# The last column block's second product in five rounds of 8 row tiles, with the closing of each group between rounds

## The chip, the cores and the metric

The kernel runs on one core of one Trainium2 chip. The metric is device time in microseconds (us) of one execution. Engines by their names in the profile: PE (TensorE, matrix product), PEld (its weight loads), DVE (VectorE), ACT (ScalarE), POOL (GpSimd), SP (SyncE, which issues most transfers here). SBUF is the on-chip memory, PSUM the accumulators that PE writes (8 banks of 512 f32 columns per partition, taken here as 4 pairs).

## The reference

`x` is 5120x64, `adj` a sparse 5120x5120 f32 matrix. What matters here, cut down:

```python
e = concat([par_u0*par_u1*(diag_u*x_u @ W_u) + x_u, par_i0*par_i1*(diag_i*x_i @ W_i) + x_i])
h = adj @ (adj.T @ e)
out = layernorm(h) * gamma + beta + x
x1 = layernorm(x + out)
result = layernorm(x1 + graph_layers(x1, adj))
```

`graph_layers` keeps edges and nodes by thresholds. A largest row-wise sum of squares of `adj` under a bound proves that nothing survives them; then the second part adds zero, and the last line is a layer norm of a layer norm. The kernel computes that maximum, stores the short answer, and branches on the flag at its very end; with these inputs the branch is not taken.

## The kernel before, in words

**Tiling.** The 5120 rows are 40 row tiles of 128. The columns of `adj` come in 11 blocks (`NB`), two of 256 columns and nine of 512. A block arrives in units of 1024 elements per partition (two row tiles of a 512-column block). For each block PE first multiplies all its tiles against `e` (`multiply_unit`, L1303, the product `adj.T @ e`). ACT sums the squares of each unit, and DVE transposes each unit in 32x32 squares (`turn_unit`, L1159). The product's two halves are transposed (`turn_half`), spread over the partitions by PE (`spread_block`, L1318) and copied to SBUF by ACT (`keep_cols`, L1069).

**Second product and rounds.** `multiply_round` (L1333) then multiplies the transposed tiles by the block's 64 columns of `adj.T @ e`. One round takes some of the row tiles: 16, 16 and 8 (`ROUND_TILES`). A round writes four PSUM banks, one for each quarter of the partitions, 32 output columns for each row tile; all 16 column groups of the block accumulate there. `add_round` (L1180) on DVE adds the four banks into `h_sum` in SBUF. So `h_sum` is complete for a row tile once the last block's round with that tile has been added. In the blocks before the last, PE alternates a round of block c with units of block c+1, so that all waits on adds lie behind other products.

**Banks.** Rounds write banks 0 to 3, the last two rounds of the program banks 4 to 7 (`round_banks`). A round waits until the round before it has been added (`round_added`); the second round of the last block waits only for one older, since it takes the other four banks.

**Closing.** The 40 tiles are closed in five groups of 8 (`GT`, `LGROUPS`). `close_tiles(k)` (L1346) multiplies 8 tiles of `h_sum` by a fixed centering matrix into a PSUM pair (`nat_of`: pairs 0, 1, 0, 1, 2). Then for each group k, with the name and line of each step:

- ACT squares the centered values: `square_c` (L1091)
- DVE sums and scales them: `sum_c` (L1209, L1211)
- POOL takes the power -0.5: `root_c` (L1022)
- DVE multiplies and adds the prepared `x`: `make_y` (L1217, L1221); the first of the two frees the PSUM pair (`t_made`)
- ACT squares again: `square_y` (L1096)
- DVE sums: `sum_y` (L1227, L1230)
- POOL takes the power: `root_y` (L1027)
- DVE scales: `make_out` (L1238)
- SP stores 256 KB (L967)

Each engine works its own list in the order that the code has; an instruction whose semaphore is late holds everything behind it on that engine. The order in which the steps of the five groups follow each other on DVE, ACT and POOL is written out by hand.

Of the kernel before, what the change touches and what calls it, by code (L numbers as in the profile page):

```python
# [7 lines left out]
def adjacency_layers_kernel(nc, x, adj, w_ui, diag, par, gamma, beta,  # L8
# [38 lines left out]
    ROUND_TILES = (16, 16, 8)  # L47
    ROUND_FIRST = (0, 16, 32)
    RPB = len(ROUND_TILES)
    NR = NB * RPB  # L50

# [28 lines left out]
    with ctx:  # L80
# [42 lines left out]
        assert ln_at + 8 * GT * D <= x_at + SLOT * ROUND_TILES[0] * CH // SLOT  # L123
# [194 lines left out]
        def units_of_round(g):  # L318

            c, j = g // RPB, g % RPB  # L320
            first, last = ROUND_FIRST[j], ROUND_FIRST[j] + ROUND_TILES[j]
            return range(UNIT_FIRST[c] + first // UNIT_TILES[c], UNIT_FIRST[c] + last // UNIT_TILES[c])
# [10 lines left out]
        def round_of_tile(t):  # L333
            return 0 if t < 16 else 1 if t < 32 else 2

        def round_of_unit(v):
            c, i = place_of_unit(v)
            return RPB * c + round_of_tile(UNIT_TILES[c] * i)

# [11 lines left out]
        def round_banks(g):  # L351

            return bank[4:8] if g >= NR - 2 else bank[0:4]

# [4 lines left out]
        def turned_of(g):  # L359

            c, j = g // RPB, g % RPB
            at, w, nt = SLOT * SLOT_FIRST[c] + WIDTHS[c] * ROUND_FIRST[j], WIDTHS[c], ROUND_TILES[j]
            return pooled[:, at:at + w * nt].rearrange("p (t b r) -> p t b r", b=w // 32, t=nt)

        def h_of(j):


            at, nt = ROUND_FIRST[j] * P, ROUND_TILES[j]
            return h_sum[:, at:at + nt * P].rearrange("p (t a r) -> p a t r", a=QUADS, t=nt)
# [571 lines left out]
        def _(sp):  # L941
            for k in range(LGROUPS):
                sp.dma_start(x_first[:, group_tiles(k), :], tile_rows(x, GT * k, GT)).then_inc(x_loaded[k], 16)
            for v in range(UNITS):
# [9 lines left out]
                if before:  # L954
                    sp.wait_ge(round_done, round_of_unit(before[-1]) + 1)
# [5 lines left out]
            sp.wait_ge(round_done, RPB * (NB - 2) + 1)  # L961
# [12 lines left out]
        def _(pool):  # L974
# [69 lines left out]
        def _(act):  # L1044
# [17 lines left out]
            def keep_cols(c):  # L1062
                act.wait_ge(cols_spread, c + 1)
                if c >= 2:
                    act.wait_ge(round_done, RPB * (c - 1))
# [53 lines left out]
        def _(dve):  # L1119
# [49 lines left out]
            def add_round(g):  # L1169
                j, w = g % RPB, 32 * ROUND_TILES[g % RPB]  # L1170
                dve.wait_ge(round_done, g + 1)
                if g >= RPB:
                    dve.wait_ge(round_added, g - RPB + 1)
                for a in range(QUADS):
                    to = h_of(j)[:, a, :, :]
                    share = round_banks(g)[a][:, 0:w].rearrange("p (t r) -> p t r", r=32)
                    if g < RPB:
# [14 lines left out]
            for g in range(NR - RPB):  # L1192
                for i, v in enumerate(units_of_round(g + RPB)):
                    if i == 1 and g % RPB == RPB - 1:
                        turn_half(g // RPB + 1)
                    turn_unit(v)
                if g == NR - RPB - 2:
# [5 lines left out]
            add_round(NR - 3)  # L1203
            add_round(NR - 2)

# [64 lines left out]
        def _(pe):  # L1270
# [51 lines left out]
            def multiply_round(g):  # L1322
                w, to, kb = 32 * ROUND_TILES[g % RPB], turned_of(g), WIDTHS[g // RPB] // 32
                pe.wait_ge(unit_turned, units_of_round(g).stop)
                if g % RPB == 0:
                    pe.wait_ge(cols_kept, g // RPB + 1)
# [102 lines left out]
```

## Time and profile before

| | us |
|---|---|
| median of 3 runs (lowest, highest) | 430.44 (429.62, 434.01) |
| the profiled execution | 430.32 |
| its span, first to last instruction | 428.5 |
| PE busy | 393.6 |
| DVE busy | 329.3 |
| ACT busy | 229.3 |
| POOL busy | 39.4 |

Starts are counted from the first instruction of the span. An engine's busy time is a sum over its instructions, not a claim that it sets the time; the chain of waits is the view that follows, from the last instruction back, what each step was released by. One f32 matmul of the program shows as two matmuls and two weight loads in the trace, so a round of 64 matmuls is x128 there.

### The profile page before, as it was taken

The page shows a single profiled execution, that of the slowest core. Times are in us where ns is not written, and L with a number is a line of the kernel's source. Part 1 is how long each engine was busy: PE and PEld are TensorE (multiplying, and loading weights), DVE is VectorE, ACT ScalarE, POOL GpSimd, SP SyncE. Part 2 cuts the span into 40 slices and gives each one's busy share as a digit, 9 for nine tenths or more (in the row PEclk, how much of TensorE's full clock was granted, in tenths as well). Part 3 has the DMA queues.
Part 4 walks back from the last instruction along what each step waited for, and adds up shares of the span by engine and source line. Part 5 has one row for each costly group of instructions (what it writes and reads, how often), then busy time and mean ns, then how long its engine had stood idle before and what let it go on. Part 6 is the DMA issues. An engine that isn't in the chain of part 4 may idle for free.

```text
span 428.5 us, 13460 instructions
## 1 busy us (share of the span) xinstructions
PE 393.6 (92%) x5872; PEld 233.0 (54%) x5872; DVE 329.3 (77%) x404; ACT 229.3 (54%) x439; POOL 39.4 (9%) x56
## 2 busy tenths in 40 slices
PE   4997999999999999999999999999899999989910
PEld 3884665555565464555546456554545655455900
DVE  1588999998796796978679697967769796953864
ACT  2368579398079239607923960990396098010310
POOL 5000000000000000000000000000000000294473
PEclk9998999999999999999999999999999999999975
DMA  7999999967795795979379597957939793000012
GB/s 232 349 349 366 386 386 386 387 244 280 271 386 170 281 377 208 351 267 363 119 284 376 212 348 268 364 193 264 392 142 342 276 365 128 2 4 2 3 49 79
DMA packets 61984, 109.84 MB, mean 256 GB/s; under 512 B 3936, under 2 KB 14304, under 8 KB 61920
## 3 DMA queue, kind: packets, MB, share of 16 engines
q1 hardware_dynamic: 61248, 108.80, 71.3%
q8 instruction: 48, 0.79, 0.8%
q10 hardware_dynamic: 672, 0.12, 0.1%
q14 instruction: 16, 0.13, 0.1%
HBM read 107.60 MB, written 1.31 MB: 254 GB/s over the span
## 4 chain that ended last, share of the span: by engine, by line
PE 89%; DVE 3%; POOL 3%; issue 2%; DMA 1%; ACT 1%; DVEq 0%
PE pair L1303 42%; PE pair L1333 41%; PE pair L1318 3%; PE pair L1288 2%; POOL pooled L1027 2%; POOL pooled L1022 2%; PE pair L1278 1%; DMA pooled<-in_x 1%; PE pair L1346 1%; DVE pooled L1217 0%; DVE pooled L1159 0%; DVE pooled L1238 0%; DVE pooled L1227 0%; DVE pooled L1178 0%; DVE pooled L1180 0%
## 5 line engine op out<-in xcount | busy, mean ns | idle before, releaser
L1159 DVE STREAM_TRANSPOSE pooled<-pooled 128x1024 f32<-128x1024 f32 x200 | 229.9, 1207 | 7.7 <-PE pair L1303 4.7
L1059 ACT ACTIVATE scratch<-pooled 128x1024 bf16<-128x1024 f32 x200 | 208.2, 1050 | 0.0
L1333 PE MATMUL pair<-pooled,col_sum 32*64 32x512 f32 (+1 forms) x3840 | 181.0, 520 | 5.3 <-issue 3.2
L1303 PE MATMUL pair<-pooled,rows_in 128*64 128x256 f32 (+1 forms) x1760 | 183.6, 367 | 0.0
L1303 PEld LDWEIGHTS pair<-pooled,rows_in 128*64 128x64 f32 x1760 | 121.3, 140 | 67.4 <-issue 18.9
L1333 PEld LDWEIGHTS pair<-pooled,col_sum 32*64 32x64 f32 x3840 | 84.3, 132 | 88.2 <-issue 81.0
L1180 DVE TENSOR_TENSOR pooled<-pooled,pair 128x512 f32<-128x512 f32 (+1 forms) x120 | 63.4, 588 | 64.9 <-PE pair L1333 64.9
L1069 ACT COPY col_sum<-pair 128x512 f32<-128x512 f32 (+1 forms) x22 | 11.0, 550 | 138.2 <-PE pair L1318 138.2
L1059 ACT ACTIVATION_READ_ACCUMULATOR scratch<-pooled 128x1 f32 x200 | 38.9, 195 | 0.0
L1008 POOL TENSOR_SCALAR pooled<-pooled 128x40 f32<-128x40 f32 x1 | 0.3, 316 | 363.3 <-DVE pooled L1199 363.3
L1318 PE MATMUL pair<-col_half,spread_cols 64*128 64x256 f32 (+1 forms) x88 | 11.6, 383 | 3.8 <-DVE col_half L1167 3.8
L1091 ACT ACTIVATE pooled<-pair 128x512 f32<-128x512 f32 x5 | 3.0, 593 | 18.8 <-PE pair L1346 18.8
L1318 PEld LDWEIGHTS pair<-col_half,spread_cols 64*128 64x128 f32 x88 | 7.2, 186 | 10.0 <-issue 5.7
L1096 ACT ACTIVATE pooled<-pooled 128x512 f32<-128x512 f32 x5 | 3.1, 630 | 14.9 <-DVE pooled L1221 14.9
L1346 PEld LDWEIGHTS pair<-center,pooled 128*128 128x128 f32 x80 | 9.1, 192 | 1.2 <-issue 1.2
L1278 PE MATMUL pair<-ident,pooled 128*128 128x128 f32 x20 | 5.0, 403 | 5.1 <-DMA pooled<-in_x 5.1
L1133 DVE TENSOR_TENSOR rows_in<-pair,pooled 128x256 f32<-128x256 f32 x10 | 3.8, 419 | 7.7 <-PE pair L1288 7.7
L1346 PE MATMUL pair<-center,pooled 128*128 128x128 f32 x80 | 9.5, 278 | 0.0
L1022 POOL TENSOR_TENSOR pooled<-pooled,minus_half 128x8 f32<-128x8 f32 x5 | 8.2, 1644 | 8.6 <-DVE pooled L1211 8.5
L1027 POOL TENSOR_TENSOR pooled<-pooled,minus_half 128x8 f32<-128x8 f32 x5 | 8.1, 1636 | 8.7 <-DVE pooled L1230 8.7
L1053 ACT COPY pooled<-pair 128x512 f32<-128x512 f32 x5 | 2.9, 585 | 11.0 <-PE pair L1278 11.0
L1288 PE MATMUL pair<-pooled 64*128 64x64 f32 x80 | 8.1, 366 | 0.6 <-ACT pooled L1053 0.6
(49 smaller groups left out, 74.8 us busy)
## 6 DMA issues: line engine op xcount, KB each, us to landing
pooled<-in_adj SPq DMA_DIRECT2D x200, 512.0 KB, 8.9
pooled<-in_x SPq DMA_DIRECT2D x5, 256.0 KB, 5.2
out<-pooled SPq DMA_DIRECT2D x5, 256.0 KB, 2.0
pooled<-in_x SPq DMA_DIRECT2D x1, 768.0 KB, 6.8
pooled<-in_x SPq DMA_DIRECT2D x1, 512.0 KB, 4.2
pooled<-in_w_ui ACTq DMA_DIRECT2D x2, 32.0 KB, 5.5
beta_sb<-in_beta ACTq DMA_DIRECT2D x1, 32.0 KB, 6.3
pooled<-in_diag ACTq DMA_DIRECT2D x1, 20.0 KB, 5.1
```

Source lines behind the costliest of these rows:

```text
L1022: nc.gpsimd.tensor_tensor(rstd[:, group_tiles(k)], var[:, group_tiles(k)], minus_half[:, :], ALU.pow).then_inc(rstd_made, 1)
L1027: nc.gpsimd.tensor_tensor(scale[:, group_tiles(k)], y_var[:, group_tiles(k)], minus_half[:, :], ALU.pow).then_inc(scale_made, 1)
L1059: nc.scalar.activation(scratch[v % 2][:, :], slots[slot_of(v)], ACT.Square, accum_out=square_sum[:, v:v + 1]).then_inc(unit_scanned, 1)
L1069: kept = act.copy(to.rearrange("p b (f i) -> p f b i", f=2), spread_bank[h][:, 0:w].rearrange("p (f b i) -> p f b i", f=2, i=32))
L1159: nc.vector.transpose(tiles, tiles).then_inc(unit_turned, 1)
L1180: added = nc.vector.tensor_tensor(to, to, share, ALU.add)
L1278: mm = pe.transpose(pair_bank(k)[:, P * j:P * j + P], x_first[:, t:t + 2, :].rearrange("p t d -> p (t d)"), ident[:, :])
L1288: mm = pe.matmul(xw_bank(k, odd)[:, t % GT // 2, :], xt_pairs[half(odd), P * (t // 2):P * (t // 2) + P], w_ui_sb[half(odd), D * w:D * w + ...
L1303: mm = pe.matmul(block_bank[c % 2][half(h), 0:w // 2], rows_in[:, t, :], slots[slot_of(v)][:, at:at + w // 2], start=(t == 0), stop=(t == ...
L1318: mm = pe.matmul(spread_bank[h][:, w * f:w * (f + 1)], spread_cols[f][half(h), :], col_half[half(h), 0:w], start=True, stop=True)
L1333: mm = pe.matmul(round_banks(g)[a][half(b % 2), 0:w].rearrange("p (t r) -> p t r", r=32), col_sum[g // RPB % 2][quadrant(a), b, :], to[qua ...
L1346: mm = pe.matmul(nat_of(k)[:, i, :], h_sum[:, P * t:P * t + P], center[:, :], start=True, stop=True)
```

## The change

The last block's rounds are five of 8 row tiles; the other ten blocks keep 16, 16 and 8. Round and group sizes in the last block are now equal: group k closes the tiles of its round k. On PE, `close_tiles(0)` stands behind round 1, `close_tiles(1)` behind round 2, `close_tiles(2)` behind round 3, and 3 and 4 behind round 4. The last block's rounds 1 to 4 all write banks 4 to 7, round 0 banks 0 to 3. The order of the closing steps on DVE, ACT and POOL is rewritten to match. The rest of the diff replaces arithmetic on round numbers by tables and changes no instruction.

```diff
-    ROUND_TILES = (16, 16, 8)
-    ROUND_FIRST = (0, 16, 32)
-    RPB = len(ROUND_TILES)
-    NR = NB * RPB
+    PARTS = ((0, 16), (16, 16), (32, 8))
+    LAST_PARTS = tuple((t, 8) for t in range(0, T, 8))
+    RPB = len(PARTS)
+    ROUNDS_AT = [RPB * c for c in range(NB)]
+    LAST = ROUNDS_AT[NB - 1]
+    NR = LAST + len(LAST_PARTS)
...
+        def place_of_round(g):
+
+            c = min(g // RPB, NB - 1)
+            return (c,) + (LAST_PARTS if c == NB - 1 else PARTS)[g - ROUNDS_AT[c]]
...
+        def rounds_through(c, t):
+
+            return next(g + 1 for g in range(NR) if place_of_round(g)[0] == c and t < sum(place_of_round(g)[1:]))
...
-            return bank[4:8] if g >= NR - 2 else bank[0:4]
+            return bank[4:8] if g > LAST else bank[0:4]
...
             root_c(0)
             root_c(1)
             root_y(0)
+            root_c(2)
             root_y(1)
-            root_c(2)
             root_c(3)
+            root_c(4)
             root_y(2)
-            root_c(4)
             root_y(3)
             root_y(4)
...
             square_y(0)
-            square_y(1)
             act.wait_ge(c_summed, 1)
             square_c(2)
+            square_y(1)
             act.wait_ge(c_summed, 2)
...
-            add_round(NR - 3)
-            add_round(NR - 2)
+            add_round(LAST)
+            add_round(LAST + 1)
...
             sum_c(0)
+            add_round(LAST + 2)
+            make_y(0)
             sum_c(1)
-            make_y(0)
+            sum_y(0)
+            add_round(LAST + 3)
             make_y(1)
-            add_round(NR - 1)
-            sum_y(0)
+            make_out(0)
+            sum_c(2)
             sum_y(1)
-            sum_c(2)
+            add_round(LAST + 4)
+            make_y(2)
+            make_out(1)
             sum_c(3)
-            make_out(0)
-            make_out(1)
-            make_y(2)
+            sum_y(2)
+            sum_c(4)
             make_y(3)
-            sum_c(4)
-            sum_y(2)
+            make_y(4)
             sum_y(3)
-            make_y(4)
             make_out(2)
+            sum_y(4)
             make_out(3)
-            sum_y(4)
...
-                if g == NR - 2:
+                if g == LAST + 1:
                     pe.wait_ge(round_added, g - 1)
                 elif g:
                     pe.wait_ge(round_added, g)
...
-                pe.wait_ge(round_added, NR - RPB + round_of_tile(GT * k) + 1)
+                pe.wait_ge(round_added, rounds_through(NB - 1, GT * (k + 1) - 1))
...
-            multiply_round(NR - 3)
-            multiply_round(NR - 2)
+            multiply_round(LAST)
+            multiply_round(LAST + 1)
             close_tiles(0)
+            multiply_round(LAST + 2)
             close_tiles(1)
-            multiply_round(NR - 1)
+            multiply_round(LAST + 3)
             close_tiles(2)
+            multiply_round(LAST + 4)
             close_tiles(3)
             close_tiles(4)
```

PE's list from the last `spread_block` on, before (L1318 spreads, L1333 is the second product, L1346 closes, L1390 is the matmul for the maximum):

```order
L1318 MATMUL pair<-col_half,spread_cols 128x256 x4
L1333 MATMUL pair<-pooled,col_sum 64x512 x128
L1346 MATMUL pair<-center,pooled 128x128 x16
L1333 MATMUL pair<-pooled,col_sum 64x256 x64
L1346 MATMUL pair<-center,pooled 128x128 x24
L1390 MATMUL pair<-ident,part_max 1x128
```

The same place in the changed kernel, whose lines are L1324, L1340, L1353 and L1399:

```order
L1324 MATMUL pair<-col_half,spread_cols 128x256 x4
L1340 MATMUL pair<-pooled,col_sum 64x256 x128
L1353 MATMUL pair<-center,pooled 128x128 x8
L1340 MATMUL pair<-pooled,col_sum 64x256 x64
L1353 MATMUL pair<-center,pooled 128x128 x8
L1340 MATMUL pair<-pooled,col_sum 64x256 x64
L1353 MATMUL pair<-center,pooled 128x128 x8
L1340 MATMUL pair<-pooled,col_sum 64x256 x64
L1353 MATMUL pair<-center,pooled 128x128 x16
L1399 MATMUL pair<-ident,part_max 1x128
```

The first two closings moved ahead of rounds, one round later each, and only two closings are left behind the last round, where there were three.

DVE's list from the add of the last round on, before:

```order
L1180 TENSOR_TENSOR pooled<-pooled,pair 128x8x32 x4
L1227 TENSOR_REDUCE pooled<-pooled 128x8
L1230 TENSOR_SCALAR pooled<-pooled 128x8
...
L1209 TENSOR_REDUCE pooled<-pooled 128x8
L1211 TENSOR_SCALAR pooled<-pooled 128x8
...
L1238 TENSOR_TENSOR pooled<-pooled 128x512 x2
L1217 TENSOR_TENSOR pooled<-pair,pooled 128x512
L1221 TENSOR_TENSOR pooled<-pooled 128x512
```

And in the changed kernel (the add is L1183, `make_y` L1221 and L1225, `make_out` L1242, `sum_c` L1213 and L1215):

```order
L1183 TENSOR_TENSOR pooled<-pooled,pair 128x8x32 x4
L1221 TENSOR_TENSOR pooled<-pair,pooled 128x512
L1225 TENSOR_TENSOR pooled<-pooled 128x512
L1242 TENSOR_TENSOR pooled<-pooled 128x512
L1213 TENSOR_REDUCE pooled<-pooled 128x8
L1215 TENSOR_SCALAR pooled<-pooled 128x8
```

Behind the last add stood two `sum_y`, two `sum_c`, two `make_out` and only then the third group's `make_y`; now that `make_y` follows the add at once.

## Rows read from the trace of the kernel before

**Rows 1.** The page: the span, an instruction queue, and the chain's shares by engine

```profile
span 428.5 us, 13460 instructions
...
q8 instruction: 48, 0.79, 0.8%
...
PE 89%; DVE 3%; POOL 3%; issue 2%; DMA 1%; ACT 1%; DVEq 0%
```

**Rows 2.** The chain of waits, 372 us to the end: start, us, what

```profile
375.16 3.64 PE pair L1333 x128
...
381.09 13.99 PE pair L1333 x256
395.08 3.78 PE pair L1346 x32
...
398.88 0.61 ACT pooled L1091
...
405.78 3.23 POOL pooled L1027 x2
409.01 3.21 POOL pooled L1022 x2
```

**Rows 3.** Busy time by stretch: PE, PEld, DVE, ACT, POOL, granted clock, DMA share, GB/s

```profile
381.00:408.10 27.10, 27.01 (x466) 18.64 (x466) 13.83 (x29) 3.65 (x6) 14.29 (x12) 1.00 0.01 2
408.10:428.50 20.40, 0.25 (x2) 0.00 (x0) 10.66 (x21) 2.37 (x4) 10.58 (x7) 0.59 0.18 67
```

**Rows 4.** DVE's timeline: start, us, instruction, idle time before it and its releaser

```profile
395.17 2.48 DVE L1180 TENSOR_TENSOR pooled<-pooled,pair 128x512 f32<-128x512 f32 x4 [4.39 <-PE pair L1333]
397.73 0.69 DVE L1209 TENSOR_REDUCE pooled<-pooled 128x8 f32<-128x512 f32 x1
398.45 0.17 DVE L1211 TENSOR_SCALAR pooled<-pooled 128x8 f32<-128x8 f32 x1
...
401.13 0.69 DVE L1221 TENSOR_TENSOR pooled<-pooled 128x512 f32<-128x512 f32 x1
...
403.49 1.40 DVE L1180 TENSOR_TENSOR pooled<-pooled,pair 128x256 f32<-128x256 f32 x4
...
423.77 0.69 DVE L1238 TENSOR_TENSOR pooled<-pooled 128x512 f32<-128x512 f32 x1 [1.39 <-POOL pooled L1027]
```

**Rows 5.** POOL's and ACT's timeline in the closing stage

```profile
398.70 3.43 POOL L1022 TENSOR_TENSOR pooled<-pooled,minus_half 128x8 f32<-128x8 f32 x2 [8.50 <-DVE pooled L1211]
418.53 1.64 POOL L1027 TENSOR_TENSOR pooled<-pooled,minus_half 128x8 f32<-128x8 f32 x1
401.86 0.63 ACT L1096 ACTIVATE pooled<-pooled 128x512 f32<-128x512 f32 x1 [2.38 <-DVE pooled L1221]
```

**Rows 6.** PE's timeline around its waits, with one add of DVE

```profile
35.88 3.47 PE L1303 MATMUL pair<-pooled,rows_in 128*64 128x128 f32 x32
50.26 1.97 PE L1303 MATMUL pair<-pooled,rows_in 128*64 128x128 f32 x32
50.44 2.48 DVE L1178 COPY pooled<-pair 128x512 f32<-128x512 f32 x4 [0.23 <-PE pair L1333]
53.07 1.99 PE L1333 MATMUL pair<-pooled,col_sum 32*64 32x256 f32 x64 [0.84 <-DVE pooled L1178]
188.44 3.70 PE L1333 MATMUL pair<-pooled,col_sum 32*64 32x256 f32 x127
193.78 0.43 PE L1333 MATMUL pair<-pooled,col_sum 32*64 32x256 f32 x1 [1.63 <-issue]
305.38 0.37 PE L1333 MATMUL pair<-pooled,col_sum 32*64 32x256 f32 x1 [1.60 <-issue]
```

**Rows 7.** Busy time by stretch, as in Rows 3, for the clock behind two idle times

```profile
31.00:35.20 4.20, 0.48 (x10) 0.24 (x6) 4.20 (x6) 3.33 (x8) 0.00 (x0) 1.00 1.10 348
35.24:39.20 3.96, 3.96 (x40) 3.59 (x40) 2.48 (x3) 3.20 (x7) 0.00 (x0) 0.62 1.09 360
...
53.07:57.00 3.93, 3.93 (x86) 2.98 (x88) 3.87 (x8) 1.25 (x3) 0.00 (x0) 1.00 1.05 386
```

More of the change, by code:

```diff
@@ L316, in place_of_unit, with units_of @@
             return c, v - UNIT_FIRST[c]
[L318 to L322, printed above, removed]
+        def place_of_round(g):
+            c = min(g // RPB, NB - 1)
+            return (c,) + (LAST_PARTS if c == NB - 1 else PARTS)[g - ROUNDS_AT[c]]
+        def units_of(c, first, nt):
+            return range(UNIT_FIRST[c] + first // UNIT_TILES[c], UNIT_FIRST[c] + (first + nt) // UNIT_TILES[c])
         def tile_rows(ap, t0, nt):
@@ L954, in _ @@
                 if before:
-                    sp.wait_ge(round_done, round_of_unit(before[-1]) + 1)
+                    b, ib = place_of_unit(before[-1])
+                    sp.wait_ge(round_done, rounds_through(b, UNIT_TILES[b] * ib))
                 sp.dma_start(slots[slot_of(v)].rearrange("p (t k) -> p t k", t=ut),
@@ L1064, in keep_cols @@
                 if c >= 2:
-                    act.wait_ge(round_done, RPB * (c - 1))
+                    act.wait_ge(round_done, ROUNDS_AT[c - 1])
                 w, kb = WIDTHS[c], WIDTHS[c] // 64
@@ L1169, in add_round @@
             def add_round(g):
-                j, w = g % RPB, 32 * ROUND_TILES[g % RPB]
+                c, first, nt = place_of_round(g)
                 dve.wait_ge(round_done, g + 1)
-                if g >= RPB:
-                    dve.wait_ge(round_added, g - RPB + 1)
+                if c:
+                    dve.wait_ge(round_added, rounds_through(c - 1, first + nt - 1))
                 for a in range(QUADS):
-                    to = h_of(j)[:, a, :, :]
-                    share = round_banks(g)[a][:, 0:w].rearrange("p (t r) -> p t r", r=32)
-                    if g < RPB:
+                    to = h_of(first, nt)[:, a, :, :]
+                    share = round_banks(g)[a][:, 0:32 * nt].rearrange("p (t r) -> p t r", r=32)
+                    if c == 0:
                         added = nc.vector.tensor_copy(to, share)
@@ L1191, in _ @@
             turn_unit(UPB[0] - 1)
[L1192 to L1195, printed above, removed]
+            for g in range(LAST):
+                c, first, nt = place_of_round(g)
+                for i, v in enumerate(units_of(c + 1, first, nt)):
+                    if i == 1 and first + nt == T:
+                        turn_half(c + 1)
                     turn_unit(v)
-                if g == NR - RPB - 2:
+                if g == LAST - 2:
                     dve.wait_ge(x_again, 16 * 2)
@@ L1322, in multiply_round @@
             def multiply_round(g):
[L1323 to L1326, printed above, removed]
-                if g == NR - 2:
+                c, first, nt = place_of_round(g)
+                w, to, kb = 32 * nt, turned_of(g), WIDTHS[c] // 32
+                pe.wait_ge(unit_turned, units_of(c, first, nt).stop)
+                if first == 0:
+                    pe.wait_ge(cols_kept, c + 1)
+                if g == LAST + 1:
                     pe.wait_ge(round_added, g - 1)
@@ L1367, in _ @@
                     pe.matmul(bank[6][:, 0:D], center_t, center_g, start=True, stop=True).then_inc(gamma_turned, 1)
-            for g in range(NR - RPB):
-                c, j = g // RPB, g % RPB
-                ahead = units_of_round(g + RPB)
-                first = 2 if c == 0 else 0
-                if j == 0:
-                    for v in ahead[:first]:
-                        multiply_unit(v)
+            for g in range(LAST):
+                c, first, nt = place_of_round(g)
+                ahead = units_of(c + 1, first, nt)
+                early = 2 if g == 0 else 0
+                for v in ahead[:early]:
+                    multiply_unit(v)
+                if first == 0:
                     spread_block(c)
-                for v in ahead[first if j == 0 else 0:]:
+                for v in ahead[early:]:
                     multiply_unit(v)
```

21 lines of the change are left out of this document (8 added, 13 removed).

## The prediction

> **What bounds the kernel now.** I read the page first. The span is 428.5 us and PE holds 89% of the chain that ended last [rows 1], so up to the last block only PE's time matters. The chain of waits, read in order of time, shows where that ends [rows 2]. The last block's first two rounds run from 381.09 us for 13.99 us, two closings follow for 3.78 us, and from 398.88 us on PE is hardly in it: the chain goes through ACT, POOL (two pairs of powers, 3.23 and 3.21 us) and DVE. The busy times by stretch say the same [rows 3]: PE is busy 27.01 of 27.10 us up to 408.10 us and 0.25 us of the 20.40 us behind. In those 20.40 us, POOL is busy 10.58 us and DVE 10.66 us, so neither is full, but they hand work to each other. The last instruction starts at 423.77 us and takes 0.69 us [rows 4]: it ends at 424.46 us, 16.4 us behind PE's last closing.
>
> The question is therefore how soon the closing chains begin, and how many stand behind PE's end. POOL's first power starts at 398.70 us, after 8.50 us of waiting [rows 5]. There are ten powers at 1.6 us each, 16 us of POOL's time, of which two were done before PE's last closings began.
>
> **The change part by part.**
>
> *The rounds.* A 512-column round is 13.99/2 = 7.00 us, an 8-tile round 3.64 us [rows 2]. The old three make 7.00 + 7.00 + 3.64 = 17.64 us, the new five 5 x 3.64 = 18.20 us: **0.6 us more** on PE. Halving the long one would give 3.50 us, the lower bound; the row of the same shape is nearer, so I take 3.64.
>
> *The adds.* An add of 16 tiles is 2.48 us, one of 8 tiles 1.40 us [rows 4]. Five are 7.0 us against 2 x 2.48 + 1.40 = 6.4 us, 0.6 us more on DVE. It waits in this stretch (4.39 us in front of one add [rows 4]), so this costs nothing by itself. Without that cover it would cost 0.6 us.
>
> *The new waits.* Rounds 2, 3 and 4 take the banks that the round before them has just left, so each waits for an add that begins only when that round ends. The wait was behind two closings, now it is behind one. A closing is 3.78/2 = 1.89 us [rows 2]. An add starts 0.1 us after its round (395.08 to 395.17 us [rows 2, 4]), takes 1.40 us, and PE resumes 0.15 us after it (50.44 + 2.48 = 52.92, then 53.07 us [rows 6]): 1.65 us. It fits under 1.89 us with **0.24 us to spare**, if DVE is free when the round ends. Queued behind the waiting round is everything on PE; queued behind a waiting add on DVE are `make_y` and `sum_c` of the group before.
>
> *The walk.* I lay out every instruction of the closing stage in its engine's written order, at its row's duration. An 8-tile `sum` gives its result after 0.88 us and holds DVE for 0.8 us (397.73 to 398.45, plus 0.17), POOL starts 0.1 us later (398.70), a power is 1.64 us and holds POOL for 1.60 us, `make_y` is 1.41 us, ACT's squares 0.61 and 0.63 us, `make_out` 0.69 us [rows 2, 4, 5]. Done for the old order, this walk ends at 424.56 us; the trace has 424.46 us. That is my reason to trust it to some tenths. For the new order:
>
> - PE: rounds end at 384.7, 388.4, 393.9, 399.4 and 405.0 us, with closings between. The last closing ends at 408.7 us (408.2 in the same walk of the old order), without a wait.
> - DVE's adds start at 384.8, 388.5, 394.0, 399.5 and 405.1 us, each as its round ends. DVE is free for each; the narrowest is the last, free 0.7 us before.
> - POOL: the powers of group 0 start at 392.0 us, not at 398.7. Those of `root_c` 1, `root_y` 0, `root_c` 2 and `root_y` 1 start at 397.6, 399.2, 403.8 and 405.4 us, so **five of ten** have begun before PE is done.
> - After PE: closing 3 ends at 406.85, its square at 407.6, its sum starts at 408.3 (behind `make_y` and `make_out`), and `root_c` 3 starts at 409.3. From 410.9 us `root_c` 4 and `root_y` 2 to 4 run nearly back to back, to 418.1 us. The last `make_out` runs from 418.13 to 418.82 us.
>
> The end of DVE's work moves from 424.56 to 418.82 us, **5.7 us earlier**. What follows it (the store, the flag, the branch) has no changed instruction and moves as a whole. So the profiled execution of 430.32 us becomes 430.32 - 5.7 = **424.6 us**. It stands 0.12 us below the median of 430.44 us, so the same number holds for a median.
>
> *What is late next.* Behind 408.7 us, one group alone needs two squares, two sums, two powers, `make_y` and `make_out`: about 8.8 us with the handovers. The walk has 10.1 us there. The other 1.3 us is POOL's queue of groups 2 and 3 ahead of group 4.
>
> *Bounds.* With 3.50 us a round, the end comes 0.7 us earlier: 423.9 us. Each delay of a round moves the end by as much, since in the walk PE is always the engine that the adds wait for. An add that starts or hands over 1 us later costs 0.76 us at each of three rounds, plus the last: 3.3 us in the walk, 427.9 us.
>
> **One rule against the change.** Two instructions of mine on DVE read two SBUF operands, the second half of `make_y` (L1221) and `make_out` (L1238), and in the new order more of them run beside a POOL power. The row of L1221 at 401.13 us ran while POOL was in its pair of powers from 398.70 us for 3.43 us, and took 0.69 us [rows 4, 5], the same as the last L1238, which ran alone. So I charge nothing. The Trainium skill, page "SBUF — State Buffer", section "SBUF: two separate sides", says that such a DVE operation and a GpSimd one share a port pair under an exclusive lock, and that the one that comes second "fully blocks". By that rule this row would have been longer or later; the trace does not agree. It is a rival below.
>
> **The rivals**
>
> - **Late adds (0.10).** DVE is strictly in order and now has sums and multiplies ahead of the adds of rounds 2 to 4; if they are late, PE waits three times. For: only 0.24 us of slack at each. Against: in the walk DVE is free 0.7 to 2.2 us before each add. With 0.5 to 1 us at each, the walk gives 426.0 to 427.9 us.
> - **A hole in PE's instruction supply (0.13).** Twice PE stood for 1.63 and 1.60 us for no reason that the trace shows, both times before the last matmul of an 8-tile round, x127 and then x1 [rows 6]. An 8-tile round uses as many instructions as a 16-tile one in half the time, and the page has a queue that brings instructions [rows 1]. Five such rounds now stand close together. For: 2 of the 9 8-tile rounds of 512-column blocks had it. Against: both fell in stretches with heavy transfers, and the last 8-tile round, with next to none (2 GB/s [rows 3]), had none. One hole costs 1.6 us: 426.2 us.
> - **The tail keeps its length (0.06).** If what bounds the end were POOL's and DVE's hand-to-hand work as such, and not its start, the 16.4 us behind PE would stay, and the time would be 430.32 + 0.6 = 430.9 us. For: POOL and DVE are each half idle there. Against: eight powers stood behind 405 us before, five stand behind 409 us now.
> - **The port lock (0.03).** Four of the DVE operations with two SBUF operands (`make_y` 3 and 4, `make_out` 2 and 3) would each wait for the rest of a power, at most 1.64 us: 424.6 + 6.6 = 431.2 us at most.
> - **The clock falls: slower (0.03).** PE now changes between rounds and closings seven times in place of three. If it idled enough between them, its clock would fall from 2.4 to 1.2 GHz. What the rows show of that: after 3.75 us of waiting before 35.24 us the granted clock of the next stretch was 0.62, and 32 matmuls took 3.47 us that took 1.97 us later, 1.76 times [rows 6, 7]; after 0.84 us of waiting it stayed 1.00 [rows 6, 7]. In the walk PE does not wait at all, and the old stretch, which changes groups too, ran at 1.00 [rows 3]. Each microsecond of PE's work at the low level costs 0.76 us, so it decides from 5.7/0.76 = 7.5 us on. With all 20.4 us behind 388.4 us at that level: 424.6 + 15.5 = 440.1 us. The Trainium skill, page "TensorE: Matmul & The Clock Gate", section "A second HAM failure mode: psum-queue depth-cycling", tells of a kernel that cycles through PSUM banks whose clock swings for such small idle times; no run here shows it.
> - **Better than the walk (0.05).** Shorter rounds, or handovers under 0.1 us: 423.6 us.
>
> **How the numbers follow.** The forecast has 0.60 and spans 423.9 to 425.7 us by the bounds above. The low end of the range is 423.6, the high end 427.2 us: it takes in the hole and most of the late adds, and leaves out about 0.15. One per cent, about what a measurement of this kernel can tell, is 426.1 us for faster and 434.7 us for slower. Faster: 0.60 + 0.05, half of the hole and a quarter of the late adds, 0.74. Slower: the clock and a little for what I have not thought of, 0.04. The same: 0.22.
>
> **What would show it.** Five rounds of about 3.64 us each, with PE's last closing near 408.7 us, confirm the first step; waits of rounds 2 to 4 on L1183 refute the 0.24 us. POOL's first power near 392.0 us and its last from 416.5 us confirm the walk. DVE's last instruction near 418.1 us confirms the sum. A closing chain that follows PE's end by over 12 us, a wait named "issue" of over 1 us inside a round, or a granted clock below 1.00 before 408 us would each make the prediction wrong.

## The result

The changed kernel takes 426.46 us (median of 20 runs, 423.8 to 432.06) against 430.28 us (median of 20 runs of the kernel before). The ratio is **0.9913, 95% interval 0.9888 to 0.9937**: 3.7 us less, between 2.7 and 4.8. The ratio leaves out three executions of the changed kernel that were more than 1.5% above its fastest. The forecast was 424.6 us in a range of 423.6 to 427.2 us, 5.7 us less. The direction and the range held; the size was half as large again as it should have been, and lies outside the interval. The prediction had also drawn a line at one per cent, and gave 0.74 to a gain beyond it and 0.22 to none that large: measured, the gain is 0.87%, between 0.6% and 1.1%, so the smaller of these chances came out. The profiled execution took 426.81 us.

Three rows of the page of the changed kernel, the answer to [rows 1]:

```profile
span 425.0 us, 13984 instructions
...
q8 instruction: 50, 0.82, 0.8%
...
PE 91%; DVE 3%; issue 2%; POOL 2%; DMA 1%; ACTq 0%; ACT 0%
```

The span fell from 428.5 to 425.0 us, 3.5 us. The chain of waits of the changed kernel, the answer to [rows 2] (L1340 is the second product, L1353 closes, L1183 adds, L1025 and L1030 are the powers, L1242 is `make_out`):

```profile
381.04 7.17 PE pair L1340 x256
388.20 1.98 PE pair L1353 x16
390.19 3.64 PE pair L1340 x128
...
401.76 3.72 PE pair L1340 x128
...
405.55 0.29 issue
405.85 1.08 DVE pooled L1183 x3
...
409.73 3.25 POOL pooled L1025 x2
...
415.30 3.62 POOL pooled L1030 x2
418.92 0.02 issue
418.95 0.69 DVE pooled L1242
```

The last block starts at 381.04 us where it started at 381.09. A short round is 3.64 us, as in the forecast. A closing is 1.98 us, not 1.89. The last operation of DVE starts at 418.95 us, not at 418.13. After it there are 425.0 - 419.64 = 5.4 us to the end of the span; before the change these were 428.5 - 424.46 = 4.0 us.

The busy times by stretch, the answer to [rows 3] (PE, PEld, DVE, ACT, POOL, granted clock, DMA share, GB/s):

```profile
388.00:409.50 21.50, 21.19 (x474) 17.93 (x466) 15.26 (x36) 4.40 (x8) 10.24 (x7) 1.00 0.04 15
409.50:425.00 15.50, 0.00 (x0) 0.00 (x0) 8.28 (x18) 1.62 (x3) 8.45 (x5) 0.65 0.19 72
```

PE is as full as before while it alternates between rounds and closings, at a granted clock of 1.00, which is 2.4 GHz. The stretch with next to nothing on PE is 15.5 us, from 20.4.

**A measure for the experiments.** The first product of the last block starts anywhere from 378.9 to 383.8 us in the profiles shown here, for reasons that lie before anything that was changed. So each profile is measured below from that start, and of each run the ratio to the kernel before, timed beside it, is given. "Slower" means that the 95% interval of that ratio lies above 1; all ratios here lie within 2% of 1.

| kernel | start of last block | to the start of DVE's last operation | to the end of the span | SyncE's waits for the last stores |
|---|---|---|---|---|
| before | 381.09 | 42.68 | 47.41 | 2.0 |
| changed | 381.04 | 37.91 | 43.96 | 3.3 |
| e1 rounds alone | 381.16 | 46.62 | 51.64 | 2.3 |
| e2 order alone | 380.96 | 38.29 | 43.04 | 1.4 + 0.7 |
| e3 flag early | 378.89 | 39.19 | 43.91 | 2.1 |
| e4 sum first | 383.54 | 37.88 | 43.86 | 3.3 |
| e5 before, flag later | 381.56 | 42.72 | 49.04 | 3.6 |
| e6 adds delayed | 383.84 | 38.19 | 43.96 | 3.1 |
| e7 best, five rounds | 380.26 | 37.41 | 42.84 | 0.6 + 1.9 |
| e8 best, old rounds | 383.09 | 38.76 | 43.61 | 2.1 |
| e9 flag and buffers | 381.27 | 38.04 | 42.83 | 2.0 |
| e10 changed, again | 383.15 | 37.77 | 43.95 | 3.5 |
| e11 order alone, again | 380.93 | 38.29 | 43.07 | 1.1 + 1.0 |
| e12 best, again | 383.13 | 37.40 | 42.57 | 0.6 + 1.9 |

The measure repeats to 0.3 us in kernels that ran twice.

### The profile page after: what moved, and what is told of

Read it like the earlier page. It is cut to its first block, busy times and chain, and to the rows that moved or that the text cites. A ratio compares the mean times of both kernels' runs of the same rounds, so it can differ in the third digit from the quotient of the medians.

```text
span 425.0 us, 13984 instructions
## 1 busy us (share of the span) xinstructions
PE 393.7 (93%) x6128; PEld 238.4 (56%) x6128; DVE 329.8 (78%) x412; ACT 229.3 (54%) x439; POOL 39.8 (9%) x56
## 4 chain that ended last, share of the span: by engine, by line
PE 91%; DVE 3%; issue 2%; POOL 2%; DMA 1%; ACTq 0%; ACT 0%
PE pair L1340 42%; PE pair L1309 42%; PE pair L1324 3%; PE pair L1294 2%; PE pair L1353 1%; DMA pooled<-in_w_ui 1%; POOL pooled L1030 1%; POOL pooled L1025 1%; PE pair L1284 1%; DVE pooled L1162 0%; DVE pooled L1181 0%; DVE pooled L1225 0%; DVE pooled L1221 0%; DVE pooled L1242 0%; DVE pooled L1183 0%
## 5 line engine op out<-in xcount | busy, mean ns | idle before, releaser
L1340 PE MATMUL pair<-pooled,col_sum 32*64 32x512 f32 (+1 forms) x4096 | 181.5, 498 | 5.5 <-issue 3.5
L1340 PEld LDWEIGHTS pair<-pooled,col_sum 32*64 32x64 f32 x4096 | 90.0, 132 | 82.6 <-issue 74.4
L1183 DVE TENSOR_TENSOR pooled<-pooled,pair 128x512 f32<-128x512 f32 (+1 forms) x128 | 64.2, 562 | 63.9 <-PE pair L1340 63.9
L1324 PE MATMUL pair<-col_half,spread_cols 64*128 64x256 f32 (+1 forms) x88 | 12.0, 392 | 3.8 <-DVE col_half L1170 3.8
L1324 PEld LDWEIGHTS pair<-col_half,spread_cols 64*128 64x128 f32 x88 | 7.5, 192 | 10.3 <-issue 5.9
L1353 PEld LDWEIGHTS pair<-center,pooled 128*128 128x128 f32 x80 | 9.2, 192 | 1.9 <-issue 1.9
L1353 PE MATMUL pair<-center,pooled 128*128 128x128 f32 x80 | 10.0, 280 | 0.3 <-issue 0.3
L1025 POOL TENSOR_TENSOR pooled<-pooled,minus_half 128x8 f32<-128x8 f32 x5 | 8.2, 1645 | 11.4 <-DVE pooled L1215 11.4
L1030 POOL TENSOR_TENSOR pooled<-pooled,minus_half 128x8 f32<-128x8 f32 x5 | 8.5, 1711 | 0.7 <-DVE pooled L1234 0.7
L1294 PEld LDWEIGHTS pair<-pooled 64*128 64x128 f32 x80 | 7.3, 270 | 2.2 <-DMA pooled<-in_w_ui 1.2
```

Source lines behind the costliest of these rows:

```text
L1025: nc.gpsimd.tensor_tensor(rstd[:, group_tiles(k)], var[:, group_tiles(k)], minus_half[:, :], ALU.pow).then_inc(rstd_made, 1)
L1030: nc.gpsimd.tensor_tensor(scale[:, group_tiles(k)], y_var[:, group_tiles(k)], minus_half[:, :], ALU.pow).then_inc(scale_made, 1)
L1183: added = nc.vector.tensor_tensor(to, to, share, ALU.add)
L1294: mm = pe.matmul(xw_bank(k, odd)[:, t % GT // 2, :], xt_pairs[half(odd), P * (t // 2):P * (t // 2) + P], w_ui_sb[half(odd), D * w:D * w + ...
L1324: mm = pe.matmul(spread_bank[h][:, w * f:w * (f + 1)], spread_cols[f][half(h), :], col_half[half(h), 0:w], start=True, stop=True)
L1340: mm = pe.matmul(round_banks(g)[a][half(b % 2), 0:w].rearrange("p (t r) -> p t r", r=32), col_sum[c % 2][quadrant(a), b, :], to[quadrant(a ...
```

## The experiments

**e1: the short rounds alone.** PE runs four rounds before the first closing; DVE, ACT and POOL close in the old order. The edit is shown against the changed kernel.

```diff
             multiply_round(LAST)
             multiply_round(LAST + 1)
-            close_tiles(0)
             multiply_round(LAST + 2)
-            close_tiles(1)
             multiply_round(LAST + 3)
-            close_tiles(2)
+            close_tiles(0)
+            close_tiles(1)
             multiply_round(LAST + 4)
+            close_tiles(2)
             close_tiles(3)
...
+            add_round(LAST + 2)
+            add_round(LAST + 3)
             sum_c(0)
             sum_c(1)
             make_y(0)
             make_y(1)
             add_round(LAST + 4)
```

> Five rounds of 8 row tiles, but the closing in the old order: PE runs rounds 0 to 3, closes groups 0 and 1, runs round 4, closes groups 2 to 4; DVE, ACT and POOL close as before the change. Theory 1 (the interleaving of closings is what makes short rounds free, because a closing of 1.9 us covers the 1.65 us between a round's end and the release of its banks): rounds 2 and 3 now wait 1.65 us each with nothing to cover it, PE's last closing ends 0.6 + 3.3 = 3.9 us later than before, and the whole is 3.9 us slower than before, about 434.2 us. Rival (the add's handover costs PE nothing, short rounds alone cost 0.6 us): 430.9 us, no wait of PE on the adds.

434.37 us, ratio 1.0106 (1.0063 to 1.0149): **slower** than before, by 4.0 us of medians where 3.9 us were expected; 4.2 us by the measure. PE's timeline of e1 (start, us, instruction, idle time before it and its releaser):

```profile
389.98 3.71 PE L1340 MATMUL pair<-pooled,col_sum 32*64 32x256 f32 x128 [1.65 <-DVE pooled L1183]
395.34 3.71 PE L1340 MATMUL pair<-pooled,col_sum 32*64 32x256 f32 x128 [1.65 <-DVE pooled L1183]
```

The uncovered handover is 1.65 us, twice, the sum that the prediction made from four rows. The closing between two rounds is what hides it in the changed kernel, where no such wait shows.

**e2 and e11: the order alone.** The old rounds and PE's old list. Only the hand-written order on DVE, ACT and POOL is new.

```diff
             root_y(0)
-            root_y(1)
             root_c(2)
             root_c(3)
-            root_y(2)
+            root_y(1)
             root_c(4)
+            root_y(2)
             root_y(3)
             root_y(4)
...
             make_y(1)
-            add_round(NR - 1)
             sum_y(0)
-            sum_y(1)
+            add_round(NR - 1)
             sum_c(2)
+            sum_y(1)
             sum_c(3)
             make_out(0)
-            make_out(1)
             make_y(2)
-            make_y(3)
             sum_c(4)
             sum_y(2)
-            sum_y(3)
+            make_y(3)
...
             make_y(4)
+            sum_y(3)
+            make_out(1)
             make_out(2)
+            sum_y(4)
             make_out(3)
-            sum_y(4)
```

The two operations for the flag stand between `make_y(3)` and `make_y(4)`, `square_c(4)` stands ahead of `square_y(2)`, and `square_c(2)` ahead of `square_y(1)`. The flag is thus made at 413.08 us, 6 us before the last `make_out`, which matters for the end of the span (see e3 and e9); the column up to DVE's last operation is the one that compares the order.

> The old rounds of 16, 16 and 8 tiles and PE's old list, with only the order of the closing steps on DVE, ACT and POOL rewritten: make_y of group 2 before the make_out of groups 1 to 3, root_c 3 and 4 ahead of root_y 2, square_c 4 ahead of square_y 2. Theory 1 (the gain comes from short rounds that let the closings begin 6.7 us sooner): little gain, at most 1 us, since POOL's first power stays near 398.7 us. Rival theory 2 (most of the gain comes from what stands first behind the last add, the order, and would have been had with the old rounds): the same walk that gave 424.6 us for before gives 420.1 us here, 4.5 us less, so about 425.8 us, as fast as the change or faster.

> The old rounds with the rewritten closing order, again, on the same chip as the changed kernel. Theory 2 (the order carries the gain, and short rounds add nothing to it): the same time as the changed kernel or up to 1.3 us less. Theory 1 (short rounds carry it): 2 us or more above the changed kernel.

425.17 us, ratio 0.9885 (0.9848 to 0.9921), and again 426.85 us, 0.9928 (0.9897 to 0.9959). **The old rounds with a new order are as fast as the change.** The chain of waits of e2:

```profile
400.36 1.65 POOL pooled L1022
...
406.46 3.59 POOL pooled L1022 x2
410.05 1.60 POOL pooled L1027
411.65 1.61 POOL pooled L1022
...
419.25 0.69 DVE pooled L1238
```

The first powers are where they were, at 398.6 us (the second is at 400.36 us), so nothing begins sooner. What is new is that the powers of `root_c` 2 and 3 start at 406.46 us. Before they stood behind both `root_y` 0 and 1 and started at 409.0 us [rows 2]. From 42.68 us to DVE's last operation, the order alone takes off 4.39 us, where the walk of it had 4.5; the whole change takes off 4.77.

**e3: the flag early.** The two operations on DVE that make the flag go from the end to behind `sum_c(4)`.

```diff
             sum_c(4)
+            dve.wait_ge(max_found, 2)
+            nc.vector.tensor_reduce(all_max[0:1, :], bank[6][0:1, 0:P], X, ALU.max).then_inc(max_found, 1)
+            dve.wait_ge(max_found, 3)
+            nc.vector.tensor_scalar(flag[0:1, :], all_max[0:1, :], LIMIT, None, ALU.is_ge).then_inc(flag_made, 1)
             make_y(3)
```

> The changed kernel with the two DVE operations that make the flag moved from the end to behind sum_c of group 4, some 7 us sooner. In the changed kernel the last store landed 3.8 us after its issue, in the kernel before 2.5 us. Theory 3 (the instruction load of the branch, which begins 2.1 us after the flag, fell together with the last store, and held a queue's last packets 1.3 us): the last store lands 2.0 to 2.5 us after its issue and the time falls by 1.0 to 1.5 us against the change, to about 425.2 us. Rival (two stores 1.6 us apart hinder each other whatever the branch does): no change of the 3.8 us, 426.5 us.

425.33 us, ratio 0.9902 (0.9868 to 0.9936). The median meets the 425.2 us that were expected, but by chance: the interval overlaps the changed kernel's, and the measure is unchanged, 43.91 against 43.96 us. The wait for the last store did fall from 3.3 to 2.1 us. What took its place is in the chain of waits of e3:

```profile
412.83 0.70 DVE pooled L1242
413.53 0.02 issue
413.55 4.44 DMA out<-pooled
...
418.08 0.69 DVE pooled L1242
```

Now the store of group 2 takes 4.44 us, and the last `make_out`, which writes the same of two output buffers, waits for it. The measure to the end alone would have refuted the theory.

**e4: the last sum first.**

```diff
-            make_out(2)
             sum_y(4)
+            make_out(2)
             make_out(3)
```

> The changed kernel with sum_y of group 4 ahead of make_out of group 2. In the changed kernel the power of root_y 3 took 2.02 us in place of 1.64; it was issued while DVE was in the make_out of group 2, which reads two SBUF operands. Theory 4 (POOL's power waits for such a DVE operation that is under way): all ten powers take 1.60 to 1.64 us, DVE's last operation starts 0.4 us sooner, 426.1 us. Rival (a stray): some power still takes about 2 us, or the same length with no gain, 426.5 us.

425.57 us, ratio 0.9897 (0.9846 to 0.9949). The timelines of POOL and DVE in the changed kernel, where two powers in a row took 3.61 us:

```profile
415.30 3.61 POOL L1030 TENSOR_TENSOR pooled<-pooled,minus_half 128x8 f32<-128x8 f32 x2 [0.73 <-DVE pooled L1234]
```

```profile
415.13 0.69 DVE L1242 TENSOR_TENSOR pooled<-pooled 128x512 f32<-128x512 f32 x1
```

And of POOL in e4:

```profile
415.56 1.64 POOL L1030 TENSOR_TENSOR pooled<-pooled,minus_half 128x8 f32<-128x8 f32 x1
417.93 3.24 POOL L1030 TENSOR_TENSOR pooled<-pooled,minus_half 128x8 f32<-128x8 f32 x2 [0.73 <-DVE pooled L1234]
```

The pair takes 3.24 us, like the pair in [rows 2], when no `make_out` is under way at its start. The 0.37 us were real. The last power ended 37.63 us after the first product of the last block, 0.25 us sooner than in the changed kernel, though PE's last closing ended 0.2 us later by the same count. It brought nothing here: the later `make_out(2)` made its store later, and the last `make_out` had to wait for that buffer (DVE stood for 0.77 us, and the store was what ended it).

**e5: the same collision put into the kernel before.**

```diff
             sum_y(4)
+            nc.vector.memset(c_sq[0], 0.0)
+            nc.vector.memset(c_sq[1], 0.0)
             dve.wait_ge(max_found, 2)
```

> The kernel before, with two fills of a free 128x512 buffer put on DVE in front of the two operations that make the flag, so that the flag comes some 0.5 to 0.8 us later while DVE waits for POOL's last power anyway (1.39 us of room). Theory 3 (the branch's instruction load and the last store collide when the flag is made 0.7 us before the last make_out, as in the changed kernel, and not when it is 1.5 us before it): DVE's last operation stays where it was, the last store now takes 3.3 to 3.8 us to land in place of 2.5, and the time rises by about 1.3 us to 431.6 us. Rival (the changed kernel's long last store comes from the store 1.6 us ahead of it): the store stays at 2.5 us and the time at 430.3 us.

431.58 us, ratio 1.0012 (0.9982 to 1.0043): by the times alone, no difference that can be told. The timeline of DVE and SyncE's waits in e5:

```profile
423.77 0.14 DVE L1266 TENSOR_SCALAR flag<-all_max 1x1 int32<-1x1 f32 x1
424.28 0.69 DVE L1238 TENSOR_TENSOR pooled<-pooled 128x512 f32<-128x512 f32 x1 [0.37 <-POOL pooled L1027]
```

```profile
SPq L387 <- DMA out<-pooled: 3.6, 1, 3.6
```

The last operation of DVE is where it was (42.72 us by the measure, from 42.68), the wait for the last store went from 2.0 to 3.6 us, and the measure to the end from 47.41 to 49.04 us. The flag is now made 0.51 us ahead of the last `make_out`, from 1.53 us. This kernel has no short rounds and its last two stores are as far apart as before, so the long store comes from when the flag is made. In the timed runs this shows only as a median 1.0 us higher, within the interval.

**e6: the adds delayed.** A small fill between the end of a round and its add.

```diff
                 dve.wait_ge(round_done, g + 1)
+                if LAST < g < LAST + 4:
+                    nc.vector.memset(scratch[0][:, 256 * (g - LAST - 1):256 * (g - LAST)], 0.0)
```

> The changed kernel with a fill of 256 bf16 elements per partition between the arrival of a round's last product and its add, for rounds 1, 2 and 3. This delays the release of the banks by the length of that fill, d. Theory (a closing covers the handover with 0.24 us to spare, as predicted): PE waits d - 0.24 us in front of rounds 2, 3 and 4, if d is over 0.24 us, and not at all if it is shorter. Rival (there is more room, since the measured closing is 1.98 us in place of 1.89): d - 0.33 us.

One run, 429.62 us, with a late start of the last block (383.84 us); 43.96 us by the measure, unchanged. DVE's timeline of e6:

```profile
396.79 0.17 DVE L1176 MEMSET scratch<- 128x128 uint32 x1 [2.25 <-PE pair L1342]
396.88 1.35 DVE L1185 TENSOR_TENSOR pooled<-pooled,pair 128x256 f32<-128x256 f32 x4
```

The add starts 0.09 us after the fill, and ends less than 0.1 us later than without one. That is less than the slack of either theory, so **inconclusive**: neither value of the slack is tested.

**e9: the early flag and a third output buffer.** The edit of e3, and:

```diff
-        ln_o = [ln_buffer(6), ln_buffer(7)]
+        ln_o = [ln_buffer(6), ln_buffer(7), ln_buffer(8)]
...
-                if k >= 2:
-                    dve.wait_ge(out_stored[k % 2], 16 * (k // 2))
+                if k >= 3:
+                    dve.wait_ge(out_stored[k % 3], 16 * (k // 3))
```

> The changed kernel with the flag made behind sum_c of group 4 and three output buffers, its order otherwise untouched. With two buffers the early flag moved the collision to the third store, for which the last make_out then waited. Theory 3: now no store that anyone waits for meets the branch's instruction load; from the first product of the last block to the end of the span it takes 42.7 us, against 43.96 us in the changed kernel, SyncE's wait for the last store is 2.0 to 2.1 us, and the time is 425.2 us. Rival (a hindered store always costs the end about 1.3 us): 43.9 us and 426.4 us.

425.53 us, ratio 0.9894 (0.9859 to 0.993). The chain and SyncE's waits of e9:

```profile
417.76 1.53 POOL pooled L1030
419.29 0.02 issue
419.31 0.69 DVE pooled L1242
```

```profile
SPq L388 <- DMA out<-pooled: 2.0, 1, 2.0
```

The measure falls from 43.96 to 42.83 us, 1.13 us, with 42.7 expected. With no one waiting for the hindered store, the collision costs nothing. The collision is still there, in the store of group 2, as the section on the prediction shows. The times of the runs are too wide to show 1.1 us by themselves: 0.9894 and the changed kernel's 0.9914 beside it (e10) have intervals that overlap.

**e7, e8, e10 and e12: all measures together, on either rounds.** In e7 and e12 three buffers, the flag made just ahead of `sum_y(4)`, and an order of DVE meant to keep powers and `make_out` apart; e8 has the same aims on the old rounds, with an order of its own and the flag behind `make_out(1)`. The edit of e7, without buffers and flag:

```diff
             make_y(1)
-            make_out(0)
             sum_c(2)
+            make_out(0)
             sum_y(1)
             add_round(LAST + 4)
             make_y(2)
-            make_out(1)
             sum_c(3)
             sum_y(2)
             sum_c(4)
             make_y(3)
+            make_out(1)
             make_y(4)
             sum_y(3)
-            make_out(2)
             sum_y(4)
+            make_out(2)
             make_out(3)
```

> The changed kernel with what the first runs showed put together: three output buffers in place of two, so that make_out never waits for a store; the flag made before the last sum_y, so that its instruction load misses the last store; make_out moved so that no DVE operation with two SBUF operands is under way when a power is issued. Theories 3 and 4 together: all powers 1.60 to 1.64 us, the last store lands 2.5 us after its issue, DVE's last operation starts near 418.1 us when PE starts the last block at 381.0 us, and the time is 424.2 us, 2.3 us under the changed kernel. If the flag and the lock were strays: 426.5 us.

> The same measures on the old rounds of 16, 16 and 8 tiles with PE's old list. Theory 2 (the order of the closing steps gives most of the gain and short rounds little): 425.0 us, 0.8 us more than the same with five short rounds, which is what the earlier start of group 2 is worth in the walk. Theory 1 (short rounds matter as such): 2 us or more above the version with five rounds.

> The changed kernel again, unaltered, on the same chip as the next two, to compare them. Ratio to before 0.991, 426.5 us, SyncE's wait for the last store about 3.3 us.

> Five rounds with the order, the flag and three buffers tuned together, again, on the same chip. If its first result of 0.983 holds, 2 to 2.5 us under the changed kernel, 424 us, and 1 us or more under the old rounds with the rewritten order.

e7 took 423.88 us, ratio 0.983 (0.9791 to 0.9868); again, as e12, 425.72 us, 0.9891 (0.9861 to 0.992). e8 took 426.14 us, 0.9869 (0.983 to 0.9909). The changed kernel beside e12 (e10) took 427.13 us, 0.9914 (0.9875 to 0.9952), and the order alone (e11) 426.85 us, 1.1 us above e12 by the medians and 0.5 us by the measure. The gap of 2 to 2.5 us to the changed kernel did not repeat: it is 1.4 us of medians, and the measure says 42.57 to 42.84 against 43.96 us, **1.1 to 1.4 us**. That is hardly more than e9 has with its flag and buffers alone (42.83 us). In e7 DVE's last operation starts 0.63 us sooner than in e9, but its last three stores lie closer together, and from the start of that operation to the end of the span it takes 5.4 us (5.2 in e12) where e9 takes 4.8. The crowding of the stores is the likely reason; no run tests it. e8 missed its 0.8 us above e7 by the medians (2.3 us) and met it by the measure (43.61 against 42.84 us), but by luck: in e8 the last power took 2.82 us of the pair in this chain, 1.2 us more than a power alone, which the forecast did not have:

```profile
417.39 4.43 POOL pooled L1027 x2
```

That power starts at 418.99 us, and two `make_out` follow each other from 419.04 us. In e7 two powers met a `make_out` all the same; POOL, then DVE:

```profile
402.40 2.01 POOL L1025 TENSOR_TENSOR pooled<-pooled,minus_half 128x8 f32<-128x8 f32 x1 [2.38 <-DVE pooled L1215]
...
411.88 1.80 POOL L1030 TENSOR_TENSOR pooled<-pooled,minus_half 128x8 f32<-128x8 f32 x1
```

```profile
402.23 0.68 DVE L1242 TENSOR_TENSOR pooled<-pooled 128x512 f32<-128x512 f32 x1
...
411.50 0.69 DVE L1242 TENSOR_TENSOR pooled<-pooled 128x512 f32<-128x512 f32 x1
```

The first has the same offset of 0.17 us and the same 2.01 us as in the changed kernel. The second starts 0.38 us into the `make_out`, and waits less.

## Why the prediction was right in sign and too large

The forecast was 5.7 us less; from the first product of the last block to the end of the span it is 47.41 - 43.96 = 3.45 us. Of the 2.3 us between them, 1.0 us was lost on the way to DVE's last operation, and 1.3 us behind it. The range was drawn for a hole in PE's supply and for late adds, and neither came; that it took in what did come, which it had not been drawn for, is luck.

**Rounds and adds: right.** Five rounds of 3.64 us, adds of 1.42 us beginning as each round ends, no wait of PE on an add. e1 shows that the handover is 1.65 us to the digit, and that a closing has to cover it. By these rows the slack was 1.98 - 1.65 = 0.33 us and not 0.24, since a closing between rounds is 1.98 us; no run tested it.

**The walk: right in shape, 1.0 us too short.** POOL's first power came at 391.82 us (392.0 in the walk), five of ten powers had begun before PE was done, and DVE's last operation was PE's start plus 37.91 us. The walk had 418.13 - 381.09 = 37.04 us, 5.74 us less than its own 42.78 for the kernel before; measured, it is 42.68 - 37.91 = 4.77 us. Of the missing 1.0 us, 0.5 us is PE (three closings that stand alone at 1.98 us in place of 1.89, and 0.3 us of "issue" in front of one, less 0.1 us for the first two rounds, which took 7.17 us and not 7.28), 0.4 us is the power at 415.30 us that took 2.0 us, and 0.1 us is the walk's own error on the kernel before.

**The port lock: dismissed too soon.** The row that I had argued from showed a DVE operation that began while a power was under way, and such operations take 0.67 to 0.69 us in every profile here. The other way round was not in the trace of before. Eleven powers, in nine of the other profiles, start 0.16 to 0.19 us into a `make_out`, and took 1.99 to 2.02 us in place of 1.64. Two start 0.38 us into one (e7 and e12), and took 1.80 and 1.79 us; two start 0.61 us into one, and took 1.64 us. So the power waits out most of what is left of the `make_out`. In e4 the power does not take longer once the `make_out` is moved, and powers that start 0.17 us into a `sum_y` (one SBUF operand) took 1.64 us. By the rule of the Trainium skill's page "SBUF — State Buffer", section "SBUF: two separate sides", whichever of the two starts first keeps the other out; the trace agrees for the power that comes second, and not for the DVE operation that does. The last power of e8 fits neither: it starts 0.05 us ahead of two `make_out` in a row and took 2.82 us, while powers 0.07 us ahead of a single one took 1.63 to 1.64. What decides there stays open. The rival's price of up to 6.6 us was far too high and its mechanism partly true.

**The step that failed: "what follows it moves as a whole".** The end after DVE's last operation has no changed instruction, but it grew by 1.3 us. SyncE's waits by length show where, in the kernel before and in the changed one:

```profile
SPq L387 <- DMA out<-pooled: 2.0, 1, 2.0
```

```profile
SPq L389 <- DMA out<-pooled: 3.3, 1, 3.3
```

The flag is made at 422.24 us in the kernel before, 1.53 us ahead of the last `make_out`, and at 418.26 us in the changed one, 0.69 us ahead. By the code PE and ACT wait for the flag and branch on it, the others when they reach the end of their lists. In all fourteen profiles a packet of 16 KB starts on the queue named "instruction" 2.0 to 2.9 us after the flag's operation, wherever that operation stands, and a second one 3.1 to 4.0 us after the first. That these are the instructions behind the branch is inferred from this timing. The DMA view of two stretches of the kernel before, 424.0 to 424.9 us and 424.9 to 426.6 us, shows the first packet and the last store:

```profile
q8 instruction: 1, 0.02, 6.5%
...
q1 hardware_dynamic: 144, 0.26, 41.3%
```

The same for the changed kernel, 420.3 to 421.9 us and 421.9 to 423.5 us:

```profile
q1 hardware_dynamic: 135, 0.25, 41.2%
q8 instruction: 1, 0.02, 6.1%
...
q1 hardware_dynamic: 9, 0.02, 4.2%
```

Before, the instruction packet lay ahead of the store. Now it starts at 420.43 us and takes 1.55 us, among the store's packets: 135 pass, and 9 follow, the last of them 1.4 us after the others. Nine are a sixteenth of the 144. e5 made this happen in the kernel before, with two fills that only delay the flag; its stretches from 425.7 and from 427.0 us:

```profile
q1 hardware_dynamic: 135, 0.25, 49.5%
q8 instruction: 1, 0.02, 8.3%
...
q1 hardware_dynamic: 9, 0.02, 3.4%
```

The nine late packets start at 421.96 us in the changed kernel and at 427.55 us in e5, and the instruction packet ends there at 421.98 and 427.56 us. In e3 and e9 it is the second packet that meets a store, that of group 2, and again nine of 144 are late and start within 0.02 us of that packet's end; in e9 nobody waits for them. The core has 16 DMA engines, so the nine are most likely the store's share on the engine that was busy with the large packet; no row names the engine.

**What the prediction did not ask.** It took from the walk that the gain comes from closings that begin 6.7 us sooner, and never walked the new order on the old rounds. e2 and e11 did: the order gives 4.4 of the 4.8 us up to DVE's last operation, although two of its powers met a `make_out` too. To the end of the span it even takes 0.9 us less than the change (43.04 against 43.96 us), but this is the earlier flag and not the order. Short rounds cost 0.6 us, and by themselves 4.2; what their earlier start adds to a good order is small: with the early flag in all of them, 42.57 to 42.84 us (e7, e9, e12) against 43.04 to 43.07, and of runs on one chip 0.9891 against 0.9928, whose intervals overlap.

**The other rivals.** Late adds and a falling clock did not happen: no wait on L1183, and 1.00 granted up to 409.5 us. Nor did the tail keep its length: from PE's last closing to the end of DVE's work it is 10.5 us, from 16.4. The hole of 1.6 us did not come. Small ones did, in the fifth short round, in most kernels with five of them: in the chain of waits of the changed kernel it took 3.72 us and the others 3.64, with 0.29 us of "issue" ahead of the closing before it, and in e7's timeline

```profile
400.58 4.24 PE L1340 MATMUL pair<-pooled,col_sum 32*64 32x256 f32 x128
```

which is 0.5 us over the 3.71 us of its neighbours. The stretches named "issue" of 1.6 us in the middle of the kernel are in nearly all profiles, unchanged.

## What to carry to other kernels

Before splitting work to let a tail start sooner, walk the tail's in-order lists with the split left out: a better order of the same steps may give all of the gain. A short handover can be free if one independent piece of work of that length stands between, and costs its full price without it. Where two results meet at the end of a program, the distance between them is part of the timing even if neither changed; count a branch's instruction load as a transfer.

## What the runs showed of the hardware

- A 16 KB packet on the instruction queue, 2.0 to 2.9 us after the flag that the engines branch on, delayed the last 256 KB store where it met it: waits of 3.1 to 3.6 us in five profiles, 1.9 to 2.3 us elsewhere, where that store is waited for in one piece. A second one gave a store of 4.44 us in e3. Nine of the store's 144 packets were late each time.
- A GpSimd power on 128x8 elements takes 1.64 us, 2.0 us if it starts 0.17 us into a VectorE operation of 0.69 us with two SBUF operands, and 1.8 us at 0.38 us. VectorE operations that start during a power keep their 0.69 us.
- A closing of 8 tiles on PE takes 1.98 us alone and 3.78 us for two in a row, so each one more is 1.80 us, and a stretch of them costs about 0.2 us once (an estimate from these two rows).
